# First scan of a four-layer network: each Runge-Kutta stage's value is summed by TensorE in PSUM with f32 products and scaled identity matrices

## What is computed

```python
def _derivative(q, p, drive, coupling, bias):
    i_couple = jnp.tanh(q) @ coupling.T
    dq = q - q ** 3 / 3.0 - p + drive + i_couple + bias
    dp = EPSILON * (q + ALPHA - BETA * p)
    return (dq, dp)

def _rk4_step(q, p, drive, coupling, bias):      # DT = 0.01, CLAMP = 20
    dq1, dp1 = _derivative(q, p, ...)
    dq2, dp2 = _derivative(q + 0.5 * DT * dq1, p + 0.5 * DT * dp1, ...)
    dq3, dp3 = _derivative(q + 0.5 * DT * dq2, p + 0.5 * DT * dp2, ...)
    dq4, dp4 = _derivative(q + DT * dq3, p + DT * dp3, ...)
    q_next = clip(q + DT / 6.0 * (dq1 + 2 * dq2 + 2 * dq3 + dq4))
    p_next = clip(p + DT / 6.0 * (dp1 + 2 * dp2 + 2 * dp3 + dp4))
```

## Time and profile before

| | us |
|---|---|
| median of 3 runs (1880.74 to 1881.89) | 1880.77 |
| the profiled execution, its time | 1882.19 |
| the profiled execution, its span | 1880.3 |
| the scan's stretch of the span, first tanh to last stage value and trace | 259.4 to 913.9 |
| PE busy in the span | 1393.2 (74%) |
| DVE busy in the span | 1341.3 (71%) |

### The profile page before, as it was taken

How to read it: one execution, slowest core, us unless ns; L and a number is a source line. 1 busy time by engine, 2 the same in 40 slices (tenths; PEclk the granted TensorE clock), 3 DMA queues, 4 the chain that set the end, 5 groups by cost and what they waited for, 6 DMA issues and landing times. The chain is left out here.

```text
span 1880.3 us, 48170 instructions
## 1 busy us (share of the span) xinstructions
PE 1393.2 (74%) x16570; PEld 1091.2 (58%) x16570; DVE 1341.3 (71%) x6938; ACT 711.5 (38%) x2888; POOL 587.6 (31%) x1592
## 2 busy tenths in 40 slices
PE   6898865555555555555559999999999669999975
PEld 4376633333333333333248888888888357777764
DVE  4357779999999999999765555655555456776754
ACT  4558822222222222222333433333333454444332
POOL 1025535555555555555241111111111121111110
PEclk8979975555555555555679999999999879899865
DMA  3000000000000000000210000100000130000000
GB/s 119 0 1 2 2 1 2 2 2 2 2 2 2 2 2 2 2 2 2 96 51 1 35 1 17 35 18 1 1 1 1 45 79 2 3 6 11 14 14 13
DMA packets 15212, 28.05 MB, mean 15 GB/s; under 512 B 1692, under 2 KB 9464, under 8 KB 14584
## 3 DMA queue, kind: packets, MB, share of 16 engines
q1 hardware_dynamic: 14528, 22.83, 3.7%
q0 software_dynamic: 272, 2.10, 0.5%
q10 hardware_dynamic: 168, 0.04, 0.0%
HBM read 20.77 MB, written 4.19 MB: 13 GB/s over the span
## 5 line engine op out<-in xcount | busy, mean ns | idle before, releaser
L795 PE MATMUL bank<-s_tanh_hi,coup_hi 128*128 128x16 f16 x2048 | 141.7, 179 | 318.9 <-ACT s_tanh_hi L786 318.9
L795 PEld LDWEIGHTS bank<-s_tanh_hi,coup_hi 128*128 128x128 f16 x2048 | 95.2, 108 | 366.2 <-ACT s_tanh_hi L786 366.2
L786 ACT ACTIVATE s_tanh_hi<-s_s 128x32 f16<-128x32 f32 x384 | 88.0, 229 | 358.6 <-DVE s_s L662 358.6
L1221 POOL TENSOR_TENSOR prob<-prob,inv 128x512 f32<-128x512 f32 x64 | 66.5, 1040 | 426.4 <-DVE inv L1187 426.4
L1107 ACT ACTIVATE prob<-bank,neg_max 128x128 f32<-128x128 f32 x256 | 90.5, 366 | 215.6 <-DVE neg_max L1156 215.6
L795 PE MATMUL bank<-s_tanh_lo,coup_hi 128*128 128x16 f16 x2048 | 141.1, 179 | 9.3 <-DVE s_tanh_lo L656 0.8
L1707 POOL TENSOR_TENSOR stage_area<-x,h 128x32 f32<-128x32 f32 x128 | 46.5, 363 | 305.4 <-DVE h_lo L1662 303.8
L795 PE MATMUL bank<-s_tanh_hi,coup_lo 128*128 128x16 f16 x2048 | 130.0, 174 | 0.0
L997 PE MATMUL bank<-x_hi,w_hi 128*128 128x512 f32 x256 | 111.5, 435 | 22.9 <-DVE w_lo L1136 21.2
L795 PEld LDWEIGHTS bank<-s_tanh_lo,coup_hi 128*128 128x128 f16 x2048 | 94.7, 107 | 48.5 <-DVE s_tanh_lo L656 18.8
L1193 DVE TENSOR_TENSOR o_lo<-bank,o_hi 128x512 fp32r<-128x512 f32 x64 | 44.3, 692 | 88.6 <-ACT o_hi L1125 88.6
(11 more groups left out here) (284 smaller groups left out, 4510.7 us busy)
## 6 DMA issues: line engine op xcount, KB each, us to landing
w_stage<-in_L_cond_qkv_w_dram SPq DMA_DIRECT2D x12, 512.0 KB, 5.1
x_tok<-in_x_dram SPq DMA_DIRECT2D x4, 512.0 KB, 5.7
ow_stage<-in_L_cond_out_w_dram SPq DMA_DIRECT2D x4, 512.0 KB, 5.5
x_in<-x SPq DMA_DIRECT2D x1, 2048.0 KB, 11.9
stage_area<-in_L_cond_ffn_w_dram SPq DMA_DIRECT2D x2, 1024.0 KB, 6.9
x<-x_in POOLq DMA_DIRECT2D x1, 2048.0 KB, 16.3
out_dram<-stage_area SPq DMA_DIRECT2D x64, 32.0 KB, 1.6
ada_w<-in_L_cond_ada_w_dram SPq DMA_DIRECT2D x1, 1536.0 KB, 12.7
```

Source lines behind the costliest of these rows:

```text
L786: A.activation(th_hi[:, :], s, ACT.Tanh).then_inc(hi_ready, 1)
L795: ins = nc.tensor.matmul(coupled[:, B * m:B * m + B], w[:, o:o + P], th[:, B * c:B * c + B], start=(first and c == 0 and m == 0), stop=(la ...
L1221: G.tensor_tensor(prob[:, grp % 2, :, :], prob[:, grp % 2, :, :], inv[:, grp % 2, :].unsqueeze(2).broadcast_to([P, HG, T]), MUL).then_inc( ...
```

## The change

`scan1` is rewritten. The value of a stage is now built in a PSUM bank of its own (`state[0]` to `state[3]`) as a sum of f32 products on PE: an identity (or a third of one) times a linear part `base` that DVE makes ahead, the coupling product (`coup_h`, or `coup_6` in the fourth stage) with tanh in f32, in the first stage also `id_q` times the step's q, and a scaled identity times the cube. The fourth stage's input is kept at half its size, so ACT reads it with a scale of 2. ACT takes tanh and the square straight from the bank, DVE makes only the cube, the linear parts and p. POOL has no work in the loop. After each stage's last product PE runs one product of zeros, f16, 512 columns, into bank 7 (`keep_busy`). In `prepare` the coupling matrix is copied once in f32 and not scaled or split.

```diff
-            dve.wait_ge(d_coup, 16)
-            V.tensor_reduce(coup_abs[:, :], coup[:, :, :].rearrange("p c n -> p (c n)"), op=ALU.max,
-                            axis=AX_X, apply_absolute_value=True).then_inc(small_out, 1)
+            dve.wait_ge(small_full, 3)
+            chain(V.tensor_copy(g.coup[:, :], bank[2][:, :]))
...
-            V.tensor_reduce(coup_top[:, :], bank[3][0:1, 0:P], op=ALU.max, axis=AX_X).then_inc(small_out, 1)
-            dve.wait_ge(small_full, 5)
-            n = chain(V.tensor_scalar(g.coup_scale[:, 3:4], bank[0][:, 0:1], 1e-30, None, ALU.max))
-            chain.wait(n)
-            for i, step in enumerate((DT / 2, DT, DT / 6)):
-                chain(V.tensor_scalar(g.coup_scale[:, i:i + 1], g.coup_scale[:, 3:4], step, None, MUL))
-            n = chain(V.reciprocal(coup_inv[:, :], g.coup_scale[:, 3:4]))
-            chain.wait(n)
-            n = chain(V.tensor_scalar(coup_n[:, :], bank[2][:, :], coup_inv[:, 0:1], None, MUL))
-            chain.wait(n)
-            n = chain(V.tensor_copy(g.coup_hi[:, :], coup_n[:, :]))
-            chain.wait(n)
-            chain(V.tensor_tensor(g.coup_lo[:, :], coup_n[:, :], g.coup_hi[:, :], SUB))
-
-            dve.wait_ge(small_full, 6)
...
-            pe.wait_ge(small_out, 3)
-            M.transpose(bank[3][0:1, 0:P], coup_abs[:, :], g.ident[:, :]).then_inc(small_full, 1)
-            pe.wait_ge(small_out, 4)
-            pe.wait_ge(consts_made, 1)
-            M.matmul(bank[0][:, 0:1], ones_row[:, :], coup_top[:, :], start=True, stop=True).then_inc(small_full, 1)
+            pe.wait_ge(small_out, 2)
...
+    idle = sb("s1_idle", [P, 512], F16)
+    coup_h, coup_6 = (sb(n, [P, C * D]) for n in ("coup_h", "coup_6"))
+    id_q, id_cube, id_cube4, id_third = (sb(n, [P, P]) for n in ("id_q", "id_cube", "id_cube4", "id_third"))
+
+    state = [g.bank[i][:, 0:W1] for i in range(4)]
...
+            STT(base[0], p, -h, drive[:, 0:W1], MUL, ADD).then_inc(base_ready, 1)
+            V.tensor_scalar(coup_h[:, :], g.coup[:, :], h, None, MUL).then_inc(matrices, 1)
+            V.tensor_scalar(coup_6[:, :], g.coup[:, :], DT / 6, None, MUL).then_inc(matrices, 1)
...
+                def cubed(stage, s, const):
+                    dve.wait_ge(sq_ready, 4 * j + stage)
+                    STT(cube, sq, const, s, ADD, MUL).then_inc(cube_ready, 1)
+
+                n2 = do(STT(yp2, p, -h * (1 - k), gh, MUL, ADD))
+                np_ = do(V.tensor_scalar(p_scaled, p, P_IN_P, None, MUL))
+                n3 = do(STT(yp3, p, -h * r, gh, MUL, ADD))
+                n4 = do(STT(yp4, p, -h * (1 - 2 * k * r), gh, MUL, ADD))
...
+                    n = do(V.tensor_scalar(q, y, CLAMP, -CLAMP, ALU.min, ALU.max))
...
+                STT(cube, sq, CLAMP * CLAMP if j else 3.0e38, q, ALU.min, MUL).then_inc(cube_ready, 1)
+                STT(base[1], q, Q_IN_S3, yp2, MUL, ADD).then_inc(base_ready, 1)
+                n1 = do(STT(pt1, q, Q_IN_P, p_scaled, MUL, ADD))
+                n3 = do(STT(u3, q, Q_IN_S4, yp3, MUL, ADD))
+                n4 = do(STT(u4, q, Q_IN_Y, yp4, MUL, ADD))
+
+                cubed(2, s2, -3.0)
+                after(n3)
+                STT(base[2], s2, -h * e, u3, MUL, ADD).then_inc(base_ready, 1)
+                after(n4)
+                n4 = do(STT(u4s, s2, S2_IN_Y, u4, MUL, ADD))
+                n1 = do(STT(pt2, s2, S2_IN_P, pt1, MUL, ADD))
+
+                cubed(3, s3, -3.0)
+                after(n4)
+                STT(base[3], s3, S3_IN_Y, u4s, MUL, ADD).then_inc(base_ready, 1)
+                after(n1)
+                n1 = do(STT(pt3, s3, S3_IN_P, pt2, MUL, ADD))
...
+                cubed(4, s4, K4)
+                after(n1)
+                n = do(STT(p_raw, s4, 2 * S4_IN_P, pt3, MUL, ADD))
...
+                n = do(V.tensor_scalar(p, p_raw, CLAMP - ALPHA / BETA, -CLAMP - ALPHA / BETA, ALU.min, ALU.max))
...
+                if j + 1 < T:
+                    STT(base[0], p, -h, drive[:, W1 * (j + 1):W1 * (j + 2)], MUL, ADD).then_inc(base_ready, 1)
...
+            G.memset(idle[:, :], 0.0).then_inc(matrices, 1)
+            for mat, factor in ((id_q, 1.0 + h), (id_cube, -h / 3), (id_cube4, -DT / 9), (id_third, 1.0 / 3)):
+                G.tensor_scalar(mat[:, :], g.ident[:, :], factor, None, MUL).then_inc(matrices, 1)
...
-                for i, s in enumerate((y, s2, s3, s4)):
-
-                    act.wait_ge(s_ready, 4 * j + i + 1)
-                    A.activation(th_hi[:, :], s, ACT.Tanh).then_inc(hi_ready, 1)
-                    A.activation(th_f, s, ACT.Tanh).then_inc(th_ready, 1)
+                for i in range(4):
+                    if i + j:
+                        act.wait_ge(full, 4 * j + i)
+                    else:
+                        act.wait_ge(init, 1)
+                    s = state[(i + 3) % 4] if i + j else y0
+                    scale = 2.0 if i == 3 else 1.0
+                    A.activation(th, s, ACT.Tanh, scale=scale).then_inc(th_ready, 1)
+                    A.activation(sq, s, ACT.Square, scale=scale).then_inc(sq_ready, 1)
 
         @block.tensor
         def _(pe):
-            def product(w, th, first, last):
+            M = nc.tensor
+
+            def keep_busy(cols):
+                M.matmul(g.bank[7][:, 0:cols], idle[:, 0:P], idle[:, 0:cols], start=True, stop=True)
+
+            def coupled(out, w):
                 for c in range(C):
                     for m in range(C):
                         o = D * c + P * m
-                        ins = nc.tensor.matmul(coupled[:, B * m:B * m + B], w[:, o:o + P],
-                                               th[:, B * c:B * c + B], start=(first and c == 0 and m == 0),
-                                               stop=(last and c == C - 1), skip_group_check=True)
-                return ins
-
-            for i in range(4 * T):
-                pe.wait_ge(hi_ready, i + 1)
-                product(g.coup_hi, th_hi, True, False)
-                product(g.coup_lo, th_hi, False, False)
-                pe.wait_ge(lo_ready, i + 1)
-                product(g.coup_hi, th_lo, False, True).then_inc(coupled_ready, 1)
+                        M.matmul(out[:, B * m:B * m + B], w[:, o:o + P], th[:, B * c:B * c + B],
+                                 start=False, stop=False, skip_group_check=True)
+
+            def add(out, matrix, tile, first, last):
+                return M.matmul(out, matrix[:, :], tile, start=first, stop=last, skip_group_check=True)
+
+            pe.wait_ge(matrices, 7)
+            for n in range(4 * T):
+                i = n % 4
+                pe.wait_ge(base_ready, n + 1)
+                add(state[i], id_third if i == 3 else g.ident, base[i], True, False)
+                pe.wait_ge(th_ready, n + 1)
+                coupled(state[i], coup_6 if i == 3 else coup_h)
+                if i == 0:
+                    j = n // 4
+                    pe.wait_ge(dve_done, ND * j + TRACE_AT)
+                    add(state[i], id_q, trace[:, W1 * j:W1 * j + W1], False, False)
+                pe.wait_ge(cube_ready, n + 1)
+                add(state[i], id_cube4 if i == 3 else id_cube, cube, False, True).then_inc(full, 1)
+                keep_busy(512)
```

More of the change, by code:

```diff
@@ L14 @@
 from contextlib import ExitStack
+import numpy as np
 import concourse.bass as bass
@@ L616, in scan1 @@
-    ND, NP = 30, 10
-    M2_AT, M3_AT = 8, 15
-    h = DT / 2
+    y0, p, p_raw, p_scaled = (tile(f"s1_{n}") for n in ("y0", "p", "p_raw", "p_scaled"))
+    sq, cube, th = tile("s1_sq"), tile("s1_cube"), tile("s1_tanh")
+    base = [tile(f"s1_base{i}") for i in range(4)]
+    yp2, yp3, yp4, u3, u4, u4s = (tile(f"s1_{n}") for n in ("yp2", "yp3", "yp4", "u3", "u4", "u4s"))
+    pt1, pt2, pt3 = (tile(f"s1_pt{i}") for i in range(3))
+    warm = sb("s1_warm", [P, 1])
+    idle = sb("s1_idle", [P, 512], F16)
@@ L620, in scan1 @@
     drive = g.drive[:, :, :, :].rearrange("p t c b -> p (t c b)")
+    h = DT / 2
+    e = h * EPSILON
+    k = e * BETA
+    r = 1.0 - k + k * k
+    P_IN_P = 1.0 - k / 3 * (1.0 + 2 * (1 - k) + 2 * r + (1 - 2 * k * r))
+    Q_IN_P = e / 3 - k / 3 * (2 * e - 2 * k * e + 2 * k * k * e)
+    S2_IN_P = 2 * e / 3 - k / 3 * (2 * e - 2 * k * e)
+    S3_IN_P = 2 * e / 3 - k / 3 * 2 * e
+    S4_IN_P = e / 3
+    f32 = lambda v: float(np.float32(v))
+    K4 = -3.0 - 6.0 / DT
+    Q_IN_S3, Q_IN_S4 = f32(1.0 - h * e), f32(0.5 + h * k * e)
@@ L622, in scan1 @@
+    S2_IN_Y, S3_IN_Y = f32(1.0 + 2 * h * k * e), f32(2.0 - 2 * h * e)
+    over2 = f32(1.0 + h) - (1.0 + h)
+    over3 = Q_IN_S3 - (1.0 - h * e)
+    over4 = Q_IN_S4 - (0.5 + h * k * e)
+    in_y4 = 0.5 * f32(-DT / 9) * K4
+    want = (2.0 - 2 * h * k * k * e + 2 * h * k * e - 2 * h * e) / 3 + 1.0 / 3 + DT / 6
+    Q_IN_Y = (want - in_y4 * (1.0 + 2 * over4)) / f32(1.0 / 3) - S2_IN_Y * (1.0 + over2) - S3_IN_Y * (1.0 + over3)
     with nc.Block() as block:
@@ L652, in after @@
                     dve.wait_ge(dve_done, n)
-                def low(stage):
```

(38 more changed lines are left out.)

126 lines of the change are left out of this document (15 added, 111 removed).

## The result

| | before | changed |
|---|---|---|
| median, us | 1881.33 (1880.74 to 1883.14) | 2729.92 (2729.82 to 2730.13) |
| span of the profiled execution, us | 1880.3 | 2728.1 |
| first tanh of the scan, us | 259.40 | 256.84 |
| stage values and trace done (start of DVE's addition to x), us | 913.96 | 1761.73 |
| a step of the scan, us | 5.11 | 11.73 |

The ratio of changed to before is 1.4508, with a 95% interval of 1.4483 to 1.4534: 45% slower, where 2747 us had been predicted. After the scan both kernels have the same 966.4 us, so the whole difference lies at or ahead of the scan's end, and the two ends of the scan are 847.8 us apart, as are the spans.

The account below looks back on a forecast made before the run. Before, a chain of hand-overs among DVE, ACT and PE; after, PE's f32 weight loads at half clock. 4 x 2.86 + 0.43 = 11.87 us a step, 1519 for 128 against 654.5, +1 outside: 2747 us, range 2600 to 2860.

Parts of the forecast that it names:

- The pair's price: Scan on PE: an f32 product is two load-matmul pairs, 0.214 us a pair at half clock, 0.112 at full.
- The first rival: Scan on PE: pairs with just-used weights or small columns cost less; at 0.047 us a pair, total 1873; chance 0.02.
- The clock: Whole scan stays at the half clock, 1.2 GHz, as before the change.
- The three mixes in the earlier trace: L430's f32 products, four 512-column f32 matmuls, and the GRU's stretches, read for when the clock rose or fell.
- The second rival: Scan: the zeros hold the full clock, a stage takes 1.62 us, total 2085; chance 0.07.
- the third: Scan: the clock rises and falls as in the GRU, half the time at each, some 2400 us; chance 0.06.
- Who waits: Scan stages: ACT waits for PE and DVE for ACT, each more than 1 us; PE has no idle time between stages.
- The sum: Scan: 2.86 us a stage, 11.87 a step, 1519 for 128 steps against 654.5, total 2747.
- The term for the zeros: Each stage: zeros product 0.43 us, less 0.21 for the hidden base load, plus 0.07 for the f16 load.
- Outside the steps: Scan start waits for POOL's matrices, +1.3 us; `prepare` gains half of at most 1.3; together +1.

Follow-up runs that it names:

- the order experiment: Changed kernel with all PE inputs in f16, DVE's four linear parts of p moved behind the first stage's cube: 1683.37 us against 1700.11 without the move.
- the mixed kernel: Changed kernel with tanh, coupling and cube in f16, base and q in f32, no zeros, p-parts behind the first stage's cube: 1736.87 us, ratio 0.9227.
- the fastest step: Changed kernel with all PE inputs in f16, p-parts behind the first cube except `yp2` ahead of the clip, no zeros: 1672.48 us, ratio 0.8884.

## Why the prediction was right

The mechanism and the sum held, step by step.

- **The pair's price.** 0.214 us was taken from the starts in the earlier trace rows; 0.213 was measured, for 128x16 and 128x32 columns alike. Taking it from other places was sound because PE and PEld were both busy all the time there. The first rival asked whether a repeated weight is cheaper: the coupling and the identities, the same in every stage, keep to 0.213. It falls.
- **The clock.** 0.50 throughout, as taken. The three mixes in the earlier trace rows were the evidence; with the clock raised first and one or four zeros a stage, it fell again. The rule of the Trainium skill that the prediction weighed ("TensorE: Matmul & The Clock Gate", "What's actually happening": throttled is the default and activity releases it) does not carry this case if activity is read as a busy PE: PE is 1400.00 of 1400.00 us busy at 0.50. The Trainium skill's load of about 107 ns, given on the same page without regard to the clock (section "LDWEIGHTS (loading the stationary operand)"), is near our f32 pair at 2.4 GHz (0.112) and half of the one at 1.2 (0.213). The second rival and the third fall.
- **Who waits.** ACT for PE more than 1 us a stage, DVE for ACT, PE without gaps: all three in the rows above. Tanh was said to be just in time: it begins 0.44 us after the cube's second matmul (0.41 taken), PE asks at 0.84 (0.71 taken), as base's two loads behind the zeros are spread over 0.41 us. The cube on DVE is 0.19 us long, not 0.25, and has 1.6 us to spare, so its size did not matter.
- **The sum.** A stage is 2.827 us, 2.86 predicted. Ten pairs take 2.133 (2.14 in the sum); the zeros with base take 0.694 instead of 0.718. With 0.007 in the ten pairs that is 0.03 us, and 512 of them are 16 of the 17 us between 2747 and 2730. The term for the zeros was the least certain of the sum, put together from two other rows and an estimate: less base's own two pairs (0.427) it is 0.267, where 0.29 had been taken. Predicted and measured for the 128 steps are 1519 and 1502.
- **Outside the steps.** +1 was predicted; of the 847.8 us the steps have 847.4 (1502.0 - 654.6), so +0.4 was measured, but of larger parts than were told. The scan begins 2.6 us earlier, since `prepare` lost more than the half of 1.3 us that was counted, and PE then waits for POOL's four matrices until 2.75 us after the first tanh, where before it was 0.28 (259.40 to 259.68). Both are of one execution each; in the other kernels, where `prepare` is the same, the first tanh comes at 255.6 to 257.7, so this term is known to about 1 us. The first load of the scan and its releaser, and the first f32 products of `prepare`, which began at 14.40 before (L251 then):

```profile
12.20 3.54 PEld L226 LDWEIGHTS bank<-condT,w_emb 128*128 128x128 f32 x16
...
259.59 0.50 PEld L723 LDWEIGHTS bank<-s_base,ident 128*128 128x128 f32 x2 [7.53 <-POOL id_third L690]
```

The parts cancel here; of the 17 us less than one comes from them.

With four zeros the theory failed and its rival came true. Three other expectations missed in size. In the order experiment the first stage came as worked out, and the second had to wait for DVE's `base`; in the mixed kernel the later stages came as worked out, and in the first `base` came too late to be loaded beside tanh: a value that is "made ahead" as long as PE is slow is late as soon as PE is quick. Without zeros the wait for tanh was priced at 0.15 us a stage, and it is 0.07.

Not settled: a version of the new round that keeps the accuracy of before, with f16 high and low parts, was not tried; two more groups of four coupling products a stage, at the 0.19 us that four f16 loads span, would take the fastest step from 3.47 us to at most 4.99, against 5.11; that is an estimate, and it leaves out the low parts of base, q and cube and the instructions that make them. Nor is it known why L635 takes 0.19 us where L662 took 0.25, both reading PSUM. L662 also reads a scale per partition (`coup_scale`), L635 a constant; whether that is it was not tested. POOL's work is not the reason: from 300 to 900 us L662 takes 0.25 us in the 351 cases beside it and in the 118 without it. How many zeros hold the clock is known only for one, four and six a stage.

## What to carry to other kernels

Before work is moved to PE because it has idle time, ask what one product costs in its own type, and count it as pairs on one stream: on this chip an f32 product was two pairs paced by the weight load (0.43 us at 1.2 GHz), and 12 pairs a stage outweighed all that DVE, ACT and POOL were spared. A long chain of small matmuls anywhere in the same trace gives that price in advance, and here it gave the clock level with it. When the bound moves, price again what used to be ready in time: here `base` on DVE.

## What the runs showed that had not been expected

- Products of zeros do count toward keeping the full clock: with six a stage it held for the whole scan, over 1330 us, with four for 58 us, with one it fell some 4.5 us behind the start of the first stage (268.1 to 272.6).
- A PE that is busy 100% of the time can be at 1.2 GHz for 1900 us on end. Once the clock had fallen in a uniform stream, it never rose again in it.
- An f32 pair costs the same with 16 and with 32 columns at both levels, 0.112 us at 2.4 GHz and 0.213 at 1.2, so the load sets the pace (without zeros PEld is busy for 1300.00 of 1300.00 us). That is a factor of 1.9, where the clock's is 2. At 1.2 GHz one zeros product of 512 columns among f32 pairs is as dear as two of them (three more a stage cost 4.107 - 2.827 = 1.28 us, 0.427 each).
